# Places from one matmul of three columns a digit, and slots of four groups in one accumulation run, in the sorting stage of a graph attention kernel

## The reference

```python
q = (x[src] @ qW).reshape(e, 4, 24)
k = (x[dst] @ kW).reshape(e, 4, 24)
v = (x[dst] @ vW).reshape(e, 4, 24)
scores = clip(einsum('ehd,ehd->eh', q, k), -10, 10)
exp_s = exp(scores)
norms = segment_sum(exp_s, src)[src]
w = exp_s / (norms + 1e-8)
res = segment_sum(w[:, :, None] * v, src).reshape(n, d)
out = layernorm(x + (x + res), axis=-1)
```

## Time and profile before

| | |
|---|---|
| median of 3 runs | 2211.66 us (2199.44 to 2214.01) |
| profiled execution: its time | 2204.64 us |
| profiled execution: span from first to last instruction | 2202.8 us |
| TensorE busy / VectorE / ACT / POOL | 1696 / 1521 / 1163 / 1035 us |
| mean granted TensorE clock | 0.864 |
| matmuls | 21980 |
| HBM read, written | 281 MB, 202 MB |

### The profile page before, as it was taken

How to read it: one execution, slowest core, us unless ns; L and a number is a source line. 1 busy time by engine, 2 the same in 40 slices (tenths; PEclk the granted TensorE clock), 3 DMA queues, 4 the chain that set the end, 5 groups by cost and what they waited for, 6 DMA issues and landing times.

```text
span 2202.8 us, 65205 instructions
## 1 busy us (share of the span) xinstructions
PE 1696.1 (77%) x21980; PEld 1587.8 (72%) x21981; DVE 1520.8 (69%) x3655; ACT 1162.7 (53%) x2254; POOL 1035.2 (47%) x963
## 2 busy tenths in 40 slices
PE   2936776777777677777767749999999999999991
PEld 2715666766666566666666649999999999999991
DVE  3696555555656555565655438888888888888887
ACT  2423333333333333333333338888888888888881
POOL 4223555555555655555555534444444444444440
PEclk9657787787878878787877779999999999999996
DMA  9315666666666656576666667777777777777751
GB/s 331 92 65 182 215 221 236 206 243 214 239 228 224 239 201 244 214 245 221 222 232 241 221 223 234 220 227 219 222 224 222 220 227 220 223 221 223 220 185 44
DMA packets 202553, 470.82 MB, mean 214 GB/s; under 512 B 41920, under 2 KB 74944, under 8 KB 196058
## 3 DMA queue, kind: packets, MB, share of 16 engines
q1 hardware_dynamic: 149100, 291.36, 43.0%
q0 software_dynamic: 47040, 164.33, 19.2%
q10 hardware_dynamic: 6384, 14.75, 1.8%
HBM read 281.07 MB, written 202.00 MB: 219 GB/s over the span
## 4 chain that ended last, share of the span: by engine, by line
PE 56%; another core or an unknown queue 15%; DVE 13%; issue 6%; ACT 5%; ACTq 2%; SPq 1%; DVEq 1%; DMA 0%; POOL 0%; POOLq 0%
PE meta L1127 11%; PE sum_bank L1127 10%; PE two_b L1046 7%; PE two_a L1046 7%; PE two_a L1145 5%; PE two_b L1145 5%; DVE work L1387 4%; ACT work L834 4%; PE one_c L1135 2%; PE one_d L1135 2%; PE one_d L1089 2%; ACTq L795 1%; DVE work L1381 1%; PE one_c L1046 1%
## 5 line engine op out<-in xcount | busy, mean ns | idle before, releaser
L586 POOL DMA_INDIRECT sorted_rows<-work x588 | 619.8, 1054 | 515.6 <-ACT work L837 248.2
L643 POOL TENSOR_TENSOR work<-work 128x576 f32<-128x576 f32 x312 | 362.9, 1163 | 501.7 <-ACT work L876 501.7
L885 ACT ACTIVATE work<-work 128x768 f32<-128x768 bf16 x312 | 402.1, 1289 | 0.0
L834 ACT ACTIVATE work<-two_a 128x768 f32<-128x768 f32 x196 | 159.2, 812 | 430.8 <-remote 251.2
L1046 PE MATMUL two_a<-work 128*128 128x192 bf16 x2352 | 275.6, 275 | 94.4 <-DVE work L1356 46.9
L1366 DVE TENSOR_TENSOR work<-sum_bank,run_col 128x3 uint32<-128x3 f32 x196 | 31.6, 161 | 409.4 <-remote 218.3
L1046 PEld LDWEIGHTS two_a<-work 128*128 128x128 f16 x2352 | 219.6, 109 | 111.9 <-issue 102.3
L1046 PE MATMUL two_b<-work 128*128 128x192 bf16 x2352 | 272.7, 275 | 32.8 <-ACT work L834 30.6
L1127 PE MATMUL meta<-work 128*128 128x100 f32 x1872 | 243.5, 280 | 43.9 <-issue 38.0
L1127 PEld LDWEIGHTS meta<-work 128*128 128x128 f32 x1872 | 222.0, 192 | 61.8 <-issue 61.6
L1046 PEld LDWEIGHTS two_b<-work 128*128 128x128 f16 x2352 | 230.0, 110 | 50.4 <-ACT work L834 40.7
(11 more groups left out here) (231 smaller groups left out, 2971.9 us busy)
## 6 DMA issues: line engine op xcount, KB each, us to landing
work<-sorted_rows SPq DMA_DIRECT2D x624, 294.0 KB, 3.0
work<-sorted_local SPq DMA_DIRECT2D x49, 1152.0 KB
work<-kv_table SPq DMA_DIRECT2D x196, 144.0 KB
sorted_rows<-pad_rows ACTq DMA_DIRECT2D x7, 2058.0 KB, 20.7
sorted_rows<-work POOLq DMA_INDIRECT x588
kv_table<-work SPq DMA_DIRECT2D x12, 576.0 KB, 3.4
work<-in_x SPq DMA_DIRECT2D x12, 192.0 KB, 3.6
out<-acc SPq DMA_DIRECT2D x4, 576.0 KB
```

The source lines that it names most:

```text
L586: pool.indirect_dma_start(out=rows_dram, out_offset=bass.IndirectOffsetOnAxis(ap=place_now[:, u, b:b + 1], axis=0), in_=payload[:, u, b * ...
L643: pool.tensor_tensor(now[:, :, 0:D].rearrange("p c (h f) -> p c h f", h=HEADS), blk[:, k, :, :, D:2 * D].rearrange("p m c (h f) -> p (m c) ...
L834: act.activation(payload[:, u, 4 * part:4 * part + 4, 0:2 * D].rearrange("p (b k) w -> p b k w", b=2), kv_ps[part], ACT.Copy).then_inc(pay ...
L885: act.activation(hot_f[:, k % HOTF], hot[:, k % HOTS].rearrange("p n c -> p c n"), ACT.Copy).then_inc(hotf_made[k % PSEM], 1)
```

## The change

The places of a group come from three matmuls instead of nine: the moving side holds the three digits side by side, so a matmul gives three columns, and VectorE sums them. The run number, which VectorE added from `run_col`, now comes from two more rows of `stair` (partition 126 holds the run's number in its block, 127 the block's first run) against ones in `step3`. VectorE writes these two rows once, ahead of everything. The slots of a quad come from eight matmuls of 200 columns instead of 32 of 50, in one accumulation run over the whole bank, and then the four that add the tiles' starts. The constants of POOL change with it.

```diff
-        run_col = sb("run_col", [P, RB], F32)
+        in_row, n = share(at, [RB, P], BF16)
+        of_row, _ = share(n, [RB, P], BF16)
+        in_col, at = share(at, [1], F32)
+        of_col, at = share(at, [1], F32)
-        dest_ps = sum_bank[:, 0:QUAD * RB].rearrange("p (u b) -> p u b", u=QUAD)
+        dest_ps = sum_bank[:, 0:QUAD * RB * 3].rearrange("p (u b d) -> p u b d", u=QUAD, b=RB)
...
+            pool.memset(step3[:], 0.0).then_inc(consts, 1)
+            pool.memset(in_col, 0.0).then_inc(consts, 1)
+            pool.memset(of_col, 0.0).then_inc(consts, 1)
...
+            for n, col in enumerate((in_col, of_col)):
+                pool.affine_select(out=col, in_=col, compare_op=ALU.not_equal, fill=1.0, base=2 - P - n,
+                                   pattern=[[0, 1]], channel_multiplier=1).then_inc(consts, 1)
+            pool.affine_select(out=step3[:], in_=step3[:], compare_op=ALU.is_ge, fill=1.0, base=P - 3,
+                               pattern=[[0, NG], [P, 3]], channel_multiplier=-1).then_inc(consts, 1)
...
+                    (in_row, [[0, RB], [1, P]], 0, 0), (of_row, [[P, RB], [0, P]], 0, 0),
...
-                    (blk_row[:], [[1, NBLK]], 0, 0), (run_col[:], [[P, RB]], 0, 1)):
+                    (blk_row[:], [[1, NBLK]], 0, 0)):
...
                     for n in range(RB):
-                        for d in range(3):
-                            mm = pe.matmul(dest_ps[:, u, n:n + 1], stair[:, u % 2, n * P:(n + 1) * P],
-                                           step3[:, bass.ds(times(pe, c, QUAD, u), 1), d],
-                                           start=(d == 0), stop=(d == 2))
+                        mm = pe.matmul(dest_ps[:, u, n, :], stair[:, u % 2, n * P:(n + 1) * P],
+                                       step3[:, bass.ds(times(pe, c, QUAD, u), 1), :].rearrange("p o d -> p (o d)"),
+                                       start=True, stop=True)
...
-                def first_slots(u):
-
-                    if u == 0:
-                        pe.wait_ge(hits_made, a1)
-                        if not zero(a):
-                            pe.wait_ge(masked_made, times(pe, a, QUAD))
+                def first_slots():
+
+                    pe.wait_ge(hits_made, a1)
+                    if not zero(a):
+                        pe.wait_ge(masked_made, times(pe, a, QUAD))
                     for n in range(COLS):
-                        pe.matmul(slots[:, u, :], below_h[:], hits[:, 0, u, n // HC, :, n % HC],
-                                  start=(n == 0), stop=False)
-                    mm = pe.matmul(slots[:, u, :], slot0[:, bass.ds(times(pe, a, QUAD, u), 1)].to_broadcast([P, P]),
-                                   ident_h[:, 0:NB], start=False, stop=True)
-                    if u == QUAD - 1:
-                        mm.then_inc(slots_made, 1)
+                        pe.matmul(slots, below_h[:], hits[:, 0, :, n // HC, :, n % HC], start=(n == 0), stop=False)
+                    for u in range(QUAD):
+                        mm = pe.matmul(slots[:, u, :], slot0[:, bass.ds(times(pe, a, QUAD, u), 1)].to_broadcast([P, P]),
+                                       ident_h[:, 0:NB], start=False, stop=(u == QUAD - 1))
+                    mm.then_inc(slots_made, 1)
...
             dve.wait_ge(consts, NCONST)
+            last = slice(P - 32, P)
+            of_run = [stair[last, n].rearrange("p (b i) -> p b i", b=RB) for n in range(2)]
+            link(dve.tensor_scalar(of_run[1], in_row[last], in_col[last], None, ALU.mult))
+            link(dve.scalar_tensor_tensor(of_run[0], of_row[last], of_col[last], of_run[1], ALU.mult, ALU.add))
+            link(dve.tensor_copy(of_run[1], of_run[0]))
...
-                    dve.tensor_tensor(place_now[:, u], dest_ps[:, u], run_col[:], ALU.add).then_inc(place_made[u % GSEM], 1)
+                    with nc.allow_low_precision(reason="whole numbers below 2**24"):
+                        dve.tensor_reduce(place_now[:, u], dest_ps[:, u], AX.X, ALU.add).then_inc(place_made[u % GSEM], 1)
```

More of the change, by code:

```diff
@@ L414, in gnn_program @@
         stored = sem("stored")
-        NCONST = 38
+        NCONST = 44
         RANK_STEPS = 10
@@ L512, in _ @@
             pool.memset(below2_h[:], 1.0).then_inc(consts, 1)
+            pool.memset(step3[:], 0.0).then_inc(consts, 1)
+            pool.memset(in_col, 0.0).then_inc(consts, 1)
+            pool.memset(of_col, 0.0).then_inc(consts, 1)
             pool.memset(pad_rows[:], 0.0).then_inc(pads_made, 1)
-            pool.wait_ge(consts, 7)
+            pool.wait_ge(consts, 10)
             for m in (ident_f, ident_b, ident_h):
@@ L542, in _ @@
             pool.memset(slot0[:], 0.0).then_inc(consts, 1)
-            pool.memset(step3[:], 0.0).then_inc(consts, 1)
             pool.memset(stair, 0.0).then_inc(consts, 1)
@@ L897, in _ @@
         def _(pe):
-            IDENT_F = 8
+            IDENT_F = 11
             pe.wait_ge(consts, IDENT_F)
@@ L1103, in emit @@
                 if a is not None:
-                    for u in range(QUAD):
-                        first_slots(u)
+                    first_slots()
                 if c is not None:
```

## The result

The changed kernel takes 2148.13 us (median of four, 2144.08 to 2152.73) where the kernel before takes 2212.84: ratio 0.9712 [0.9669, 0.9755]. It is faster, by 64.7 us where 182 were forecast. The profiled execution took 2144.08 us, its span is 2142.3 us, 60.5 less than before.

A forecast was written before the change was run, and what follows sets the result against it. No engine was full; late reports of TensorE's work and waits bound the sorting stage. Quads falling from 22.5 to 18.7 us, times 48, took 182 off 2204.6, giving 2022; plus 7 us, 2029, say 2030. Range 1935 to 2160 us.

The forecast's parts named there:

- rival 2: Sorting stage: the hold belongs to memory traffic, not matmuls, so only the direct gain stays: about 2160 us; chance 0.16.
- The hold: Sorting stage: TensorE's work reported late and its next work let in late, twice a quad, a small one and a large.
- hold mostly gone: The forecast case in the sorting stage: 17.4 to 20.3 us a quad, 1960 to 2105 us; chance 0.60.
- near witness: A traced quad that met no large hold, its sort ending 19.1 us after the one before, with the old slots.
- The slots, 0.75 us: Slots' matmuls on TensorE, eight of 200 columns and four: 1.05 us in place of 1.79, 0.75 less a quad.
- The bound on the other side: Slots: if the strided read sets the spacing, 200 columns take 0.19 us, the whole 1.9, nothing gained.
- What is late next: Quad's limits without the hold: VectorE's chain 17.4 us, POOL 16.5, DMA 14.4, TensorE 17.4; with 1.3 added, 18.7.
- The small hold: The hold while a quad's second group is evacuated; `place(1)` taken as 0.29 us late.
- The low clock: TensorE's 1.2 GHz level at each quad's start, kept in the sum: VectorE's chain 17.4 us, without it 15.4.
- POOL's 16.5 us: Sorting stage: twelve scatters a quad, 1.059 us each and 0.32 between them, take 16.5 us.
- Rival 1: Sorting stage: high clock holds, hold gone, POOL's 16.5 us sets the pace: 1917, with 7 us added 1924; chance 0.12.
- the direct gain alone: Shorter slots (0.75 us) and places (0.15) on a quad's chain, about 0.9 us; alone 0.9 to 1.2, 50 us off.

The follow-up runs named there:

- one half of the change alone: The kernel before with only the places' part of the change (three matmuls, the sum, constants), slots as before: 2269.5 us, ratio 1.0289.
- p_one: The changed kernel with one POOL scatter a group in place of three: 1801.6 us, 0.8167 of the kernel before, in a session with the hold.
- d_two: The changed kernel with two of the three parts of k and v, 36 payload matmuls a quad fewer: 2127.5 us, ratio 0.9668.
- g_more: The changed kernel with the places' three matmuls issued three times over: 2197.3 us, 0.9952 of the kernel before.
- e_skip2: The changed kernel with every scattered row but row 0 sent out of bounds, in a session with the hold: 2130.4 us, ratio 0.9636.
- c_flat: The changed kernel with the slots' moving side read as it lies in memory, without a stride: 2182.6 us, 0.9878 of the kernel before.
- b_one: The kernel before with one POOL scatter a group in place of three, in a session without the hold: 1809.6 us, ratio 0.9509.
- f_brow: The changed kernel reading back a quarter of the broadcast of local rows, in a session without the hold: 1907.1 us, ratio 1.0009.
- h_gate: The changed kernel with POOL held ahead of a quad's last three scatters until the sort is reported, session without the hold: 1920.1 us, ratio 1.0071.
- the halves: The kernel before with the places' part of the change alone, 2269.5 us (1.0289), and with the slots' part alone, 2196.9 us (0.9962).
- the four kernels of one session: Changed kernel with scatters out of bounds (1.0056 of before); f_brow (1.0009); the places' half with POOL's last scatters held for the sort (1.0031); h_gate (1.0071).
- p_trio: The changed kernel with four scatters a quad, placed 0, 3, 0, 1 over the groups, session without the hold: 1798.5 us, ratio 0.9450.
- p_32: The changed kernel with all twelve scatters a quad, each taking 32 partitions in place of 128: 2210.6 us, 1.0019 of the kernel before.
- after2: The changed kernel, unchanged, run again in a later session with the hold: 2145.4 us, 0.9708 of the kernel before.

## Why the prediction was wrong

The sign was right, the range held the time (the top of it), and the size was off by a factor of 2.8. Neither was earned by the mechanism: one half of the change alone is slower, and the top of the range came from rival 2. By its own steps:

- **The hold was seen, and read wrong.** "It isn't the count alone; scatters go on only in the sorting stage" stood in the text, and then the sum took the hold to go with TensorE's 48 pairs. What the runs showed in its place: the same TensorE work without the hold (p_one), 36 pairs less with the hold in place (d_two, 0.4 us a quad at most), 24 pairs more for 1.0 us a quad (g_more), hardly any scattered traffic with the hold in place (e_skip2). It goes with POOL's scatter instructions. The step that failed is the one from 22.5 to 18.7 us a quad, "hold mostly gone" for 48 pairs less; the quad came to 21.5. Over the 16.6 us that twelve scatters take without the hold it costs, by my estimate (22.6 and 21.5 less 16.6), 6.0 us a quad in the kernel before and still 4.9 in the changed one. The "near witness" of 19.1 us was no typical quad either: of the 35 quads before from 300 to 1100 us one is that short, and the next is the longest of all.
- **The slots, 0.75 us.** The bound on the other side was the true one. I took the spacing of the sort's 36 columns as the same as that of the slots' 50. It isn't: 16 in 0.77 us less 0.20 for the last one's end is 0.038 us each, eight in 0.54 us less 0.21 is 0.047. And 50 strided columns at 0.9 ns are 0.045 us, the spacing that I had before me. In c_flat, which reads without the stride, they came at 1.15 us with the start rows at the high clock (532.81 to 533.96), near what I had worked out, and gave nothing.
- **What is late next.** VectorE's chain of 17.4 us was before's quad with its large waits taken off; the small holds were left in, and the low clock. With the hold gone a quad takes 14.44 us (p_one) or 14.66 (b_one). Three terms were too long. The small hold is larger than the 0.29 us that I took for it: that is VectorE's idle time, and the matmuls of `place(1)` had ended at 710.01, 1.8 us ahead of it. The low clock was kept: in p_one TensorE still waits for VectorE in every quad, yet the granted clock is 0.99 (0.82 in the kernel after), so what the forecast drew from the rule on the clock was wrong. And TensorE's 9.5 matmuls a microsecond was its rate under the hold, no limit: p_one lets through 165 in 14.44 us, 11.4 a microsecond. POOL's 16.5 us was right: 16.6 to 16.7 in the kernels with twelve scatters and no hold. Rival 1 names what sets the pace there, and 1907 to 1920 us (f_brow, h_gate) are near what it gave (1924); but it needs a session without the hold, and then the kernel before has it as well.
- **Rival 2** gave 2160 for "the direct gain alone", near the 2148 measured, by a wrong reason: the hold isn't the traffic, and the direct gain is 0.23 us a quad, not 0.9. The rest of the 65 us I put down to how the holds fall on another order of the same work. That is argued, not shown: the halves (+65 and -8 us against the kernel before) and c_flat (-22) only show how far small changes of TensorE's work carry, and I can't say for a given order what it will be.
- **Right:** `place` 162 ns (0.17 taken), places of a group 0.22 us (0.27 taken), the attention stage, and the constants under their cover. Start of the kernel after on ACT, and VectorE's first projection (40.07 in the earlier trace rows):

```profile
2.90 32.79 ACTq L807 DMA_DIRECT2D sorted_rows<-pad_rows  x7
```
```profile
40.67 0.76 DVE L1181 TENSOR_TENSOR work<-two_a,work 128x576 f32<-128x576 f32 x1 [13.69 <-ACT work L792]
```

Of the signs that I named for a hold that is gone, two came: the sort in under 3 us, and `place(3)` without its wait. Three didn't: the unknown queue under 8% (15%), POOL and VectorE over 65% (60% and 59%), the slots in 1.0 to 1.2 us (1.70). Of the signs against me two came, the quad above 21 us and the slots above 1.6 us. A reader who takes "sort fast and `place(3)` prompt" for "hold gone" is misled: the report of the sort, 1.3 to 7.9 us late at ACT's line 856, and the longer waits of `place(0)` and `place(2)` are what took their place.

The Trainium skill, NOTIFIC — the notification-queue block, section 7.1, on a block that can stall an engine, was read in the prediction as a price by TensorE's instructions. p_one has as many of these as the changed kernel and no hold; no run shows the block itself.

## What to carry to other kernels

When a profile shows late reports and engines that wait for nothing in it, find by an experiment what they go with before giving them a price; taking away most of one engine's instructions at a time, with nothing else changed, is a few lines of edit here and told what a page of sums did not. Work taken off a path that waits for something else can come back as waiting: here 0.75 us a quad off TensorE gave some 34 us more. And a sign that names one wait doesn't tell of the others: look at all waits of a kind together. The lever of this kernel is POOL's scatter instructions: with a third of them the changed kernel takes 1802 us in a session with the hold, and both kernels about 1800 without it (that is a bound, since two thirds of the rows were left out; each instruction here takes one place a partition, so fewer of them would need longer runs of edges).

## What the runs showed of the hardware

- The same program, the kernel before, takes 2193 to 2232 us in some sessions and 1898 to 1910 in others. It can be compared only within one session; the four kernels of one session and p_trio, made to tell of the hold, told nothing of it.
- In a session with the hold, ACT and VectorE start on TensorE's work up to 7.9 us after it ended while POOL issues 12 indirect scatters a quad of 21.5 us. With 4 a quad no wait is put down to it (p_one); with next to no row written (e_skip2) or a quarter of the partitions in each (p_32) it stays.
- A moving side read at every fourth 16-bit element costs 0.89 ns a column at either clock (eight of 200 columns start in the 1.42 us from 719.78 to 721.20, at 1.00, and from 611.28 to 612.70, at 0.53); read in order, eight stand in 0.85 us at the high clock and 1.49 at the low, against 1.60. The Trainium skill, SBUF — State Buffer, Door 1: The DMA port swizzle, in its note on lines of 16 bytes, says that a stride of up to 8 elements of bf16 is free; by it the slots would have taken 0.85 us. For this read of TensorE it isn't so, and the measurement decides.
- POOL's indirect scatter of 128 rows takes 1.05 to 1.10 us and 0.30 to the next; with 32 partitions still 0.93. Most of it is the price of the instruction: out of bounds or not, 1.07 (e_skip2, 1.08 in after2).
